# The end of the first attention and the start of the first expert: an earlier first gather, turned rows in the attention's own block, and a later clearing of semaphores

## What is computed

```python
for e in range(E):                       # 8 experts, cap = 640
    match = topk_experts == e            # each token has two experts
    elig = match.any(-1) & ~fallback
    pos = jnp.cumsum(elig) - 1
    kept = elig & (pos < cap)
    overflow = elig & (pos >= cap)
    slot = jnp.where(kept, pos, cap)
    idx = jnp.zeros((cap + 1,), jnp.int32).at[slot].set(tok_ids)[:cap]
    y_e = _ffn(x_flat[idx], W1[e], b1[e], W2[e], b2[e])
    y_flat = y_flat.at[idx].add(y_e * w[:, None])
    y_flat = jnp.where(overflow[:, None], y_fb, y_flat)
    fallback = fallback | overflow
```

## Time and profile before

| what | us |
|---|---|
| median of 3 runs | 848.25 (846.9 to 849.19) |
| the profiled execution's own time | 846.92 |
| its span, first to last instruction | 845.2 |
| the first attention ends, rows of L130 | 162.7 |
| the first experts' first W1 matmul | 173.37 |
| the first experts' last scatter-add is issued | 416.1 |

### The profile page before, as it was taken

The page is one execution under the profiler, slowest core; times in us unless marked ns, Lnnn a source line. Parts: engine busy times, 40 slices in busy tenths (PEclk is TensorE's granted clock), DMA queues, the critical chain, the costliest instruction groups (busy, mean ns, idle before and its releaser), DMA issues. The chain is left out here.

```text
span 845.2 us, 14866 instructions
## 1 busy us (share of the span) xinstructions
PE 634.7 (75%) x4843; PEld 473.2 (56%) x4843; DVE 513.2 (61%) x1772; ACT 415.3 (49%) x810; POOL 345.8 (41%) x478
## 2 busy tenths in 40 slices
PE   6998898289999999999523778877977730158994
PEld 5787786248768767877411445544544420046773
DVE  1575666666666575564106667779775618866752
ACT  2444431165785686577111466556755611046772
POOL 2433343465347337542312443344533312034754
PEclk9998999679999999999855798889988955569999
DMA  5461233355464455542311222223200014015643
GB/s 162 145 201 51 76 103 123 85 155 145 89 143 105 95 124 113 140 79 27 49 51 32 59 77 65 71 69 91 86 33 28 26 39 150 0 59 145 153 109 38
DMA packets 73873, 75.95 MB, mean 90 GB/s; under 512 B 8037, under 2 KB 66449, under 8 KB 73553
## 3 DMA queue, kind: packets, MB, share of 16 engines
q1 hardware_dynamic: 61217, 59.32, 22.7%
q0 software_dynamic: 10928, 15.57, 11.0%
q10 hardware_dynamic: 1664, 0.27, 0.2%
HBM read 52.20 MB, written 22.94 MB: 89 GB/s over the span
## 5 line engine op out<-in xcount | busy, mean ns | idle before, releaser
L1896 DVE CUSTOM_DVE_ANT_0 c_sn<-c_ps_s,k_mask 128x128 f32<-128x128 f32 (+1 forms) x256 | 75.8, 352 | 55.0 <-PE c_ps_s L2034 54.8
L1420 PE MATMUL b_ps_y<-b_w2h,b_hh 128*128 128x256 f16 x320 | 87.3, 273 | 4.7 <-DVE b_xl L1313 4.4
L1230 POOL DMA_INDIRECT res<-b_y,b_s_idx x40 | 73.4, 1834 | 41.6 <-ACT b_y L1272 31.8
L1728 POOL TENSOR_SCALAR_AFFINE_SELECT c_pr<-c_pr 128x512 f32<-128x512 f32 x64 | 42.8, 669 | 110.0 <-ACT c_pr L1787 109.0
L1420 PE MATMUL b_ps_y<-b_w2h,b_hl 128*128 128x256 f16 x320 | 87.2, 273 | 0.0
L1420 PE MATMUL b_ps_y<-b_w2l,b_hh 128*128 128x256 f16 x320 | 87.2, 273 | 0.0
L1304 DVE TENSOR_TENSOR b_hl<-b_h,b_hh 128x640 f16<-128x640 f32 x64 | 52.9, 826 | 39.2 <-ACT b_hh L1252 39.0
L1216 POOL DMA_INDIRECT e_xg<-rows,e_g_idx x35 | 36.9, 1056 | 83.5 <-DVE e_g_idx L1331 73.0
L2062 PE MATMUL c_ps_v<-c_pr,k_vx 128*64 128x256 f32 (+1 forms) x512 | 64.3, 378 | 5.5 <-POOL c_pr L1728 4.8
L1385 PE MATMUL b_ps_h<-b_xh,e_w1h 128*128 128x320 f16 x256 | 57.1, 305 | 3.1 <-ACT b_h L1247 2.1
L1787 ACT ACTIVATE c_pr<-c_ps_t 128x768 f32<-128x768 f32 x64 | 51.7, 807 | 13.8 <-PE c_ps_t L2048 13.8
(11 more groups left out here) (400 smaller groups left out, 1768.1 us busy)
## 6 DMA issues: line engine op xcount, KB each, us to landing
e_w<-in_L_ffn_W_dram SPq DMA_DIRECT2D x16, 1024.0 KB, 5.5
d_w<-in_L_ffn_W_down_dram SPq DMA_DIRECT2D x8, 640.0 KB
k_ks<-kT SPq DMA_DIRECT2D x48, 64.0 KB, 2.9
c_qs<-q SPq DMA_DIRECT2D x48, 64.0 KB, 2.3
d_w<-in_L_ffn_W_up_dram SPq DMA_DIRECT2D x4, 682.0 KB, 5.3
rows<-a_rows SPq DMA_DIRECT2D x8, 264.0 KB, 2.8
rows<-c_rows SPq DMA_DIRECT2D x8, 264.0 KB, 2.2
a_x_in<-in_x_dram SPq DMA_DIRECT2D x8, 256.0 KB, 3.5
```

The lines of the kernel that those rows point to most:

```text
L1230: pool.indirect_dma_start(out=dram["res"], out_offset=bass.IndirectOffsetOnAxis(ap=s_idx[u][:, j:j + 1], axis=0), in_=y[:, j, :], in_offse ...
L1420: last = pe.matmul(ps_y[(j + CT) % 2][:, 0:D], a, b[:, f, :], start=(f == 0 and k == 0), stop=(f == FC - 1 and k == 2))
L1728: pool.affine_select(out=late, in_=late, compare_op=ALU.is_ge, fill=0.0, base=0, pattern=[[0, 2], [0, 2], [1, P]], channel_multiplier=-1). ...
L1896: dve.tensor_tensor_reduce(sn[r][:, a:b], ps_s[:, r, a:b], mask[:, a:b], -1.0, 3.0e38, ALU.add, ALU.min, mx[g % 2][:, q, r, j:j + 1]).then ...
```

## The change

It touches the end of the first attention and the first step of the first experts.

- Each expert's loop on DVE works from the counts in PSUM: one comparison (`counts <= FULL`) multiplied by what was free and matched gives the next eligibility, another the new `free`. For that `tri` gets MARK + 1 on its diagonal, so that an eligible token's own count is raised by MARK = 2047 and a token that is not eligible stays under the bound. The exclusive sum comes directly from a shifted scan. f32 copies, `pos` and `over` are gone: 4 DVE instructions an expert in place of 7.
- Expert 0's slots, tables and indices are made inside the loop, between the other experts' (`first_slots`, `first_parts`, two halves of `low_parts`, `first_rows`); its tokens' numbers come without the factor `free`, and are computed again with it later for the scatter.
- POOL starts expert 0's gather after key part 4 in place of 7. Key parts 5 to 7 stand behind it.
- Expert 0's rows are turned, evicted and split in the attention's block; gates and bias are copied there too. Step -1 of the experts' block only gathers expert 1 and does the fills and loads.
- ACT evicts keys twice (f32 and f16), POOL's copy is gone; ACT waits for the store of n-2.
- PE: keys(3) is cut in halves around the last block's turn, its logits come ahead of values(3); keys(4) and later products go into and behind the loop.
- The attention's semaphores are not cleared at its end but with the experts' ones: no clearing and no second barrier between the two stages.

```diff
-        sem = stage_semaphores(nc, ctx, "a_")
+        held = keep["held"] = []
+        def sem(name):
+            held.append(nc.alloc_semaphore("a_" + name))
+            return held[-1]
...
+            pool.memset(elig[:], 0.0).then_inc(s_ecst, 1)
+            pool.affine_select(out=tri[:], in_=tri[:], compare_op=ALU.not_equal, fill=MARK + 1.0, base=0,
+                               pattern=[[-1, P]], channel_multiplier=1).then_inc(s_ecst, 1)
...
-                pool.tensor_copy(kh[u][:], kT[u][:]).then_inc(s_kh, 1)
-                after(pool, s_kh, n)
...
-            for n in range(4, B):
-                key_parts(n)
+            key_parts(4)
             pool.wait_ge(s_gi, 1)
...
+            for n in range(5, B):
+                key_parts(n)
...
+                landed(act, s_kst, n, u, 2, 32)
+                for dst in (kT[u], kh[u]):
+                    for c in range(C):
+                        last = act.activation(dst[:, c, :], bank_k[u][:, c * T:(c + 1) * T], ACT.Identity,
+                                              bias=cols["L1_xattn_bk"][:, c:c + 1])
...
             for high in up:
                 act.activation(high[1], high[0], ACT.Copy, scale=WS0).then_inc(s_wh1, 1)
+            keys(B - 1)
+            for j in range(CT):
+                act.wait_ge(s_px, j + 1)
+                act.activation(xh[:, :, j * P:(j + 1) * P], ps_xg[j % 2], ACT.Copy).then_inc(s_xh, 1)
...
+            def still_free(e):
+                dve.wait_ge(s_free, e + 1)
+                dve.scalar_tensor_tensor(out=free[:], in0=counted(e), scalar=FULL, in1=free[:], op0=ALU.is_le,
+                                         op1=ALU.mult).then_inc(s_free, 1)
             def eligible(e):
+                if e == 0:
+                    dve.tensor_copy(elig[:, 0, 1:], match[:, :, 0]).then_inc(s_elig, 1)
+                else:
+                    dve.wait_ge(s_fm, e)
+                    dve.wait_ge(s_ppos, e)
+                    dve.scalar_tensor_tensor(out=elig[:, e, 1:], in0=counted(e - 1), scalar=FULL, in1=fm[:],
+                                             op0=ALU.is_le, op1=ALU.mult).then_inc(s_elig, 1)
+                dve.tensor_tensor_scan(excl[:], one_row[:], elig[:, e, 0:NT], 0.0, ALU.mult, ALU.add)\
+                    .then_inc(s_excl, 1)
                 if e:
+                    still_free(e - 1)
+                if e + 1 < E:
+                    dve.wait_ge(s_free, e + 1)
+                    dve.tensor_tensor(fm[:], match[:, :, e + 1], free[:], ALU.mult).then_inc(s_fm, 1)
...
                 if e == 0:
                     gate_values(B - 1, 1)
+                    values(3)
                 if e == 1:
+                    first_slots()
+                if e == 2:
+                    first_parts()
+                if e == 3:
+                    low_parts(0, slice(0, NT // 2), s_atl0)
+                if e == 4:
+                    low_parts(0, slice(NT // 2, NT), s_atlo)
+                if e == 5:
+                    values(4)
+                if e == 6:
+                    first_rows()
...
             for e in range(E):
                 positions(e)
+                if e < 2:
+                    keys_half(4, e)
+                if e == 2:
+                    values(4)
+                if e == 3:
+                    keys(5)
+                if e in (5, 6):
+                    if e == 5:
+                        token_rows(ps_first, 0).then_inc(s_pfirst, 1)
+                    values_half(5, e - 5)
+                if e == 7:
+                    keys_half(6, 0)
+            keys_half(6, 1)
+            values(6)
+            keys(7)
             values(7)
...
+            pe.wait_ge(s_g[0], 16 * CT)
+            for j in range(CT):
+                if j >= 2:
+                    pe.wait_ge(s_xl, j - 1)
+                for c in range(C):
+                    last = pe.transpose(ps_xg[j % 2][:, c, :], tiles["xg"][0][:, j, c * P:(c + 1) * P], ident[:])
+                last.then_inc(s_px, 1)
...
-        sem = stage_semaphores(nc, ctx, "b_", sems.values())
+        sem = stage_semaphores(nc, ctx, "b_", (*sems.values(), *keep["held"]))
...
-                step(-1, 1, False, True, False)
+                step(-1, 1, False, False, False)
```

More of the change, by code:

```diff
@@ L268, in attention_causal @@
         s_g = [sems["g0"], sems["g1"]]
+        s_px, s_xh, s_xl, s_xgate, s_xb1 = (sems[n] for n in ("px", "xh", "xl", "gate", "b1"))
+        MARK = 2047.0
+        FULL = CAP + MARK
+        assert N <= MARK + 1
         def pipeline(step):
@@ L575, in _ @@
             residual_normalised(B - 1, 1)
+            residual_turned(B - 1, 1)
             keys(3)
-            residual_turned(B - 1, 1)
             second_exp(B - 1, 1)
-            for n in range(4, B):
+            for n in range(4, B - 1):
                 keys(n)
@@ L811, in _ @@
-            low_parts(0)
-            values(7)
-            rows_of(0)
-            high_parts(1)
-            low_parts(1)
+            dve.tensor_tensor(at_hi[1][:], tile_no[:].unsqueeze(1).to_broadcast([P, NT, CT]),
+                              hi16[:, 1, :].unsqueeze(2).to_broadcast([P, NT, CT]), ALU.is_equal)\
+                .then_inc(s_athi, 1)
+            dve.wait_ge(s_athi, 2)
+            dve.tensor_tensor(vhi[1][:], at_hi[1][:], value[:, 1, :].unsqueeze(2).to_broadcast([P, NT, CT]),
+                              ALU.mult).then_inc(s_vhi, 1)
@@ L816, in _ @@
+            low_parts(1, slice(0, NT), s_atlo)
+            values(6)
             for k, low in enumerate(up):
@@ L976, in half_product, with keys_half, values_half, token_rows @@
                 return last
+            def keys_half(n, r):
+                if r == 0:
+                    after(pe, s_kT, n, 2)
+                last = half_product(bank_k[n % 2], wkT1, cT[n], r)
+                if r == 1:
+                    last.then_inc(s_pk, 1)
+            def values_half(n, r):
+                if r == 0:
+                    after(pe, s_v, n, 2)
+                last = half_product(bank_v[n % 2], cT[n], wvT1, r)
+                if r == 1:
+                    last.then_inc(s_pv, 1)
             def positions(e):
-                out = ps_pos[:, e * NT:(e + 1) * NT]
-                pe.wait_ge(s_e16, e + 1)
-                pe.matmul(out, tri[:], elig16[:, e, :], start=True, stop=False)
+                out = ps_pos[e % 2][:, (e // 2) * NT:(e // 2 + 1) * NT]
+                pe.wait_ge(s_elig, e + 1)
+                pe.matmul(out, tri[:], elig[:, e, 1:], start=True, stop=False)
                 pe.wait_ge(s_excl, e + 1)
                 pe.matmul(out, ones16[:], excl[:], start=False, stop=True).then_inc(s_ppos, 1)
-            def token_rows(e):
-                pe.wait_ge(s_vhi, e + 1)
-                pe.wait_ge(s_atlo, e + 1)
+            def token_rows(out, e):
                 for i in range(NT):
-                    last = pe.matmul(ps_idx[e][:, 0:CT], at_lo[e][:, i, :], vhi[e][:, i, :],
-                                     start=(i == 0), stop=(i == NT - 1))
-                last.then_inc(s_pidx, 1)
+                    last = pe.matmul(out, at_lo[e][:, i, :], vhi[e][:, i, :], start=(i == 0), stop=(i == NT - 1))
+                return last
             pipeline(step)()
@@ new lines, in _ @@
+                if e == 7:
+                    keys_half(6, 0)
+            keys_half(6, 1)
+            values(6)
+            keys(7)
+            values(7)
+            pe.wait_ge(s_vhi, 1)
+            token_rows(ps_idx[0], 0).then_inc(s_pidx, 1)
+            pe.wait_ge(s_vhi, 2)
+            pe.wait_ge(s_atlo, 2)
+            token_rows(ps_idx[1], 1).then_inc(s_pidx, 1)
+            pe.wait_ge(s_g[0], 16 * CT)
+            pe.wait_ge(s_b1T, 1)
+            for j in range(CT):
+                if j >= 2:
[3 more added lines that the diff above has]
+                last.then_inc(s_px, 1)
@@ L1156, in step @@
                     load_down(e + 1)
-                if rows and not (isinstance(e, int) and e + 2 >= E):
+                if rows and not (isinstance(e, int) and e + 2 >= E) or isinstance(e, int) and e == -1:
                     sp.wait_ge(s_wl1, (e + 2) * WP)
```

197 lines of the change are left out of this document (103 added, 94 removed).

## The result

The changed kernel takes 834.65 us, the median of 4 runs (833.27 to 837.94), against 847.58 for the kernel before in the same comparison: a ratio of 0.985 (95% interval 0.982 to 0.989), 12.5 us. The forecast was 835.3 in 831.5 to 841.0. The profiled execution took 833.27, its span is 831.6.

What follows compares the result with a forecast made beforehand. One chain bounds the stretch: DVE's expert loop, expert 0's tables, gather, turned rows, W1, up to the W2 products. 846.92 - 13.5 (W2 earlier) + 0.6 (clearing) = 834.0; with 1.33 to the median, 835.3, range 831.5 to 841.

Steps and rivals of the forecast that it cites:

- A: The forecast as summed over the attention's end and first expert: 834 to 837.5 us, likeliest 835.3, chance 0.50.
- `Match` stayed in place: Up to the last block's `match`: 0 us change, staying at 131.1, with bounds of 0.8 to either side.
- The indices: End of DVE's expert loop: expert 0's indices at 141.4 in place of 155.95, 14.5 us earlier, bounds 12.5 and 15.
- The gather: Expert 0's five gathers on POOL: from 142.4 to 149.9, with 1.5 us of holding by DVE, bounds nothing and 8.4.
- E: Gather starved beside DVE: each piece held as the first was, 6.9 us over the sum, 842.2; chance 0.03.
- The wait for the key store: Behind the gather, ACT's keys(7) wait for key part 5's store to land at 154.2; the wait the change adds.
- Expert 1's rows: In expert 0's W1 products: gather ends at 169.25, rows land at 172.6, PE waits behind group 3 from 171.
- 837.2: Key part 5 held until DVE's four `w1l` end at 152.1, by the shared-port lock: sum 1.9 us longer.
- Rival B: In expert 0, POOL's f16 memsets hold DVE instructions until 174.6, W2 at 183.8: 838.3 us; chance 0.16.
- The clearing at the end: Semaphore clearing at the experts' end, bare behind the last scatter-add: adds 0.6 us, bounds 0.1 and 1.0.
- C: Attention's block ends later (held gathers, PE at 1.2 GHz in the loop, late store): 3 to 5 us, 838.3 to 840.3; chance 0.18.
- D: Better: gathers unheld, no wait behind group 3, loop at its near bound: 3 us less, 832.3; chance 0.10.

Runs made afterwards that it cites:

- e5: Changed kernel with POOL copying the keys to f16 (`kh`) again and ACT evicting them once: 834.25 us, ratio .983 to the kernel before.
- e0: The changed kernel run again, unaltered: 837.1 us, ratio .987 to the kernel before.
- e2: Changed kernel with expert 0's gather put behind key parts 5 to 7 again: 843.03 us, ratio .993 to the kernel before.
- e1: Changed kernel with POOL doing key part 5 ahead of expert 0's gather: 835.99 us, ratio .986 to the kernel before.
- e7: Changed kernel with key part 5 ahead of expert 0's gather and expert 1's gather at the attention block's end: 834.18 us, ratio .984 to the kernel before.
- e9: The kernel of e7 (two alterations to the changed kernel) run once more: 834.57 us, ratio .984 to the kernel before.
- e3: Changed kernel with the attention's semaphores cleared at its end again, with the second barrier: 839.81 us, ratio .988 to the kernel before.
- e6: Changed kernel with expert 1's gather issued at the end of the attention's block: 835.57 us, ratio .985 to the kernel before.
- e8: Changed kernel with `kh` on POOL, key part 5 ahead of the gather and expert 1's gather in the attention's block: 834.61 us, ratio .984 to the kernel before.
- e4: Changed kernel with expert 0's rows turned, evicted and split in the experts' block again: 836.97 us, ratio .988 to the kernel before.

## Why the prediction was right

It was right in sign, size and mechanism (A). Step by step, predicted and measured:

| step | predicted | measured |
|---|---|---|
| DVE's first step of the loop | 131.1 | 131.5 |
| expert 0's indices | 141.4 | 142.4 |
| gather, start and end | 142.4, 149.9 | 143.4, 150.6 |
| keys(7) start on ACT | 154.3 | 154.7 |
| POOL's part 7 done | 157.1 | 157.7 |
| block over | 160.7 | 161.4 |
| first W1 product | 161.2 | 161.9 |
| expert 1's gather ends | 169.25 | 170.5 |
| expert 1's rows land | 172.6 | 172.8 |
| fifth gelu | 174.6 | 174.9 |
| W2 products | 180.8 | 181.4 |
| gain at W2 | 13.5 | 13.2 by the marks |
| added at the experts' end | 0.6 | 1.3 to 1.6 |

- **`Match` stayed in place** (18.12 after the softmax, 17.94 before), though POOL's `kl` (129.73, 1.15) holds a DVE cast to 1.00; the forecast had it hold the one-hot comparisons right behind that cast. With one eviction on ACT (e5) it comes 1.0 earlier, so the new order of the products gives about 1.0 back; that was not measured by itself.
- **The indices came 1.0 late**: the loop started 0.4 later (131.53, of which 0.3 is the later softmax) and took 10.91 in place of 10.3. DVE waits for the positions behind PE's whole products after experts 2 and 3, 0.27 (at 135.88) and 0.73 (at 138.43), and was 0.4 faster elsewhere. I took these products to lie beside DVE's work, and at the high clock they do:

```profile
135.63 2.65 PE L924 MATMUL a_ps_v<-a_wvT,a_w_all 128*128 128x256 f32 x8
...
138.43 0.18 DVE L760 SCALAR_TENSOR_TENSOR a_elig<-a_ps_c,a_fm 128x16 f16<-128x16 f32 x1 [0.73 <-PE a_ps_c L1080]
```

The product took 2.65 in place of 1.97 at a clock of 0.50 to 136 us and 0.75 from there to 138. In e0, the same kernel at 1.00 there, both products take 1.97, DVE waits for neither, and the loop takes 10.34, though a scan of 0.19 takes 0.94 beside POOL's part. So this is the case that the forecast had as a bound, PE at 1.2 GHz, and it comes in some executions only.

- **The gather.** 7.17 against 7.5: one piece held by 0.95, where 1.5 was taken. E put 1.68 on each, and the whole gather was held by 1.2, so it falls. e2 shows its new place to be the largest part, 6.2 of 11.6.
- **The wait for the key store** came as described, with 5.69 on ACT. By e1 it is worth 2.3 us. That DVE's values(7) wait in the same way wasn't in the forecast; e5, with the turned rows behind that wait alone, ends its block at 48.0 after the softmax in place of 48.2.
- **Expert 1's rows** landed on time by luck. The gather ended 1.25 later than forecast, since `at_lo` held its first piece to 164.15 in place of 163.3 and its fourth took 1.45 in place of 0.95, but PE went on 2.3 behind its end, where I took 3.4 from expert 0's.
- **POOL and DVE.** The forecast weighed whether key part 5 is held by the four `w1l` until 152.1. It went the other way: POOL's two parts took 2.27, as elsewhere, and the `w1l` 5.00, where e1 has 2.58 for them. That fits the lock that the Trainium skill ("SBUF — State Buffer", section "SBUF: two separate sides") describes, if it is granted anew for each instruction: 2.58 + 2.27 = 4.85. The forecast's 837.2 by that page read it as held over all four.
- **Rival B falls.** `hl` at 171.78, beside the f16 memsets (from 170.49 on), takes 0.82 as it does elsewhere.
- **The clearing at the end was mis-sized.** I forecast 0.6 by the length of the clear alone, which is right (873 against 261 ns). The drain (0.19 longer) and the late last scatter-add (0.70) were not in the sum.
- **C** came in small, 0.6 us at W2, with one of its conditions, PE at 1.2 GHz, for 3 us of the loop. With D's 3 us nothing in the changed kernel agrees, but e7 and e9 show where they lie: in the two waits that the forecast named.

The marks give 11.6 us, the sum 12.9; the ratios give 12.5 and, in e0, 10.7. That the forecast lies within 0.7 of the first median is so far luck by about 1 us: its gain was 1.3 too large by the marks.

The single effects add up: gather's place 6.2, turning 3.2, clearing 1.8, together 11.2 of 11.6. Some 0.4 of the 1.8 is the slow `fallen` of e3. Each was undone alone from the changed kernel, so what two of them share can be counted twice or not at all. With e2's end 5.4 ahead of the kernel before, and turning and clearing worth 4.6 to 5.0, the early indices alone are left with 0.3 to 0.7. The old loop with all else new wasn't tried.

## What to carry to other kernels

Work that ends a stage early helps only from the place in a queue where it is issued: move the transfer together with the result it waits for, and count what then stands behind it. A wait whose removal brings nothing isn't yet harmless: look at the marks ahead of it, since the edit may have cost on another chain what it gave on this one, and alter the pair before deciding. When gains are 1 to 3 us and executions differ by as much, compare marks counted from a common point ahead of the change, and pair executions whose marks ahead of it agree.

## What the runs showed that was not expected

- An instruction of 0.17 us on DVE can cost 1.1 when it falls beside POOL's subtraction: the cast in the changed kernel (1.00), `fm` in e1 (1.15), `fallen` in e3 and e6 (1.13). Moving an instruction on POOL by 1 us changes which one is hit, and with the same code ahead, 0.05 us between the two starts went with a hit (e3, e6) and 0.01 with none (the changed kernel, e4).
- One kernel's executions differ by more than most edits: e0 and the first profile are 5.0 us apart at the softmax, e7 and e9 3.3 in the rest. With it goes a clock that falls to its 1.2 GHz level for a while in some executions and not in others: 0.53 to 0.56 in the 3 us from 9 us ahead of the softmax in e0, e3, e8 and e9, 1.00 in the other profiles. Those four reach the softmax at 114.5 to 118.2, the others at 110.3 to 113.2.
- POOL's indirect DMAs run past the block's barrier (e6): without a clearing, no drain waits for them. Before, the drain took 2.435.
